# Four turned tiles of the adjacency matrix left unstored in the first stage and turned again by VectorE in the passes

## The reference

```python
h = relu(layernorm(x));  e = h + par * (diag * h) @ W            # W, diag, par: one set for users, one for items
x = x + layernorm(adj @ (adj.T @ e)) * gamma + beta + h          # layer 0
h = relu(layernorm(x));  x = x + adj @ h                         # layer 1
h = relu(layernorm(x))                                           # layer 2, Chebyshev, K = 3
t1 = adj @ h;  t2 = 2 * (adj @ t1) - h;  t3 = 2 * (adj @ t2) - t1
x = x + h @ w0 + t1 @ w1 + t2 @ w2 + t3 @ w3 + bias
h = relu(layernorm(x));  d = (sum(adj + I, axis=1)) ** -0.5      # layer 3
x = x + relu((d * (adj + I) * d) @ (h @ W + b))
```

## Time and profile before

| | us |
|---|---|
| median of three runs | 1450.97 |
| the profiled execution, its own time | 1449.24 |
| its span, first to last instruction | 1447.0 |
| TensorE matmul busy | 1419.3 (98%) |
| VectorE busy | 491.5 (34%) |
| ScalarE busy | 399.7 (28%) |
| GpSimd busy | 84.2 (6%) |
| DMA, bytes moved | 523.26 MB, mean 362 GB/s |

### The profile page before, as it was taken

How to read it: one execution, slowest core, us unless ns; L and a number is a source line. 1 busy time by engine, 2 the same in 40 slices (tenths; PEclk the granted TensorE clock), 3 DMA queues, 4 the chain that set the end, 5 groups by cost and what they waited for, 6 DMA issues and landing times.

```text
span 1447.0 us, 18473 instructions
## 1 busy us (share of the span) xinstructions
PE 1419.3 (98%) x7601; PEld 600.1 (41%) x7601; DVE 491.5 (34%) x1082; ACT 399.7 (28%) x885; POOL 84.2 (6%) x67
## 2 busy tenths in 40 slices
PE   6999999999999999999999999999999999999998
PEld 3555555555555563333333333333333333333332
DVE  6684544545546533331132211011311121101044
ACT  2378777777776551000000000000000000000000
POOL 2210000000000037000000000000000000000000
PEclk9999999999999999999999999999999999999999
DMA  9999999999999998999996797899797848996998
GB/s 322 392 417 411 420 412 414 419 408 415 401 406 372 388 403 348 419 421 420 420 413 217 315 361 291 327 350 319 302 340 263 311 180 354 393 382 224 357 420 315
DMA packets 97607, 523.26 MB, mean 362 GB/s; under 512 B 18764, under 2 KB 18804, under 8 KB 54644
## 3 DMA queue, kind: packets, MB, share of 16 engines
q1 hardware_dynamic: 90436, 520.40, 91.3%
q10 hardware_dynamic: 7088, 1.67, 0.5%
HBM read 415.88 MB, written 106.17 MB: 361 GB/s over the span
## 4 chain that ended last, share of the span: by engine, by line
PE 61%; DMA 2%; DVE 1%; POOL 0%; issue 0%; ACT 0%; DVEq 0%
PE turned L640 33%; PE acc L640 25%; DMA over_wide<-adj_t 2%; PE turned L673 1%; PE turned L825 1%; PE t_rows L809 0%; PE turned L831 0%; DVE staged L1169 0%; PE t_acc L799 0%; PE t_acc L725 0%; PE t_rows L725 0%; POOL rstd L1272 0%; DVE staged L1035 0%; DVE staged L1025 0%; DVE staged L1231 0%
## 5 line engine op out<-in xcount | busy, mean ns | idle before, releaser
L1129 DVE STREAM_TRANSPOSE staged<-raw 32x256 f32<-32x256 f32 x448 | 194.9, 435 | 5.8
L651 PE MATMUL t_acc<-raw,E 128*64 128x384 f32 (+1 forms) x1120 | 184.4, 476 | 5.7 <-DMA raw<-in_adj_dram 5.7
L879 ACT ACTIVATE staged<-turned 128x512 f32<-128x512 f32 x303 | 152.7, 640 | 105.7 <-PE turned L673 105.2
L923 ACT ACTIVATE t_t<-raw 128x768 uint8<-128x768 f32 (+1 forms) x216 | 177.2, 902 | 0.0
L640 PE MATMUL acc<-staged,t_cur 128*64 128x512 f32 x720 | 161.1, 596 | 0.0
L673 PE MATMUL turned<-ident,raw 128*128 128x128 f32 x1376 | 160.2, 274 | 0.0
L673 PEld LDWEIGHTS turned<-ident,raw 128*128 128x128 f32 x1376 | 149.7, 140 | 24.9 <-issue 24.9
L640 PE MATMUL turned<-over_last,C 128*64 128x512 f32 x672 | 152.1, 592 | 0.0
L651 PEld LDWEIGHTS t_acc<-raw,E 128*64 128x64 f32 x1120 | 78.3, 138 | 109.4 <-issue 86.0
L1272 POOL TENSOR_TENSOR rstd<-rstd,minus_half 128x8 f32<-128x8 f32 (+1 forms) x30 | 44.2, 1473 | 1267.1 <-DVE rstd L1031 1267.1
L640 PE MATMUL turned<-over_last,R 128*64 128x512 f32 x512 | 116.5, 593 | 0.0
(11 more groups left out here) (139 smaller groups left out, 1062.9 us busy)
## 6 DMA issues: line engine op xcount, KB each, us to landing
over_last<-adj_t SPq DMA_DIRECT2D x181, 1024.0 KB, 8.9
staged<-adj_t SPq DMA_DIRECT2D x91, 1024.0 KB, 9.5
raw<-in_adj_dram SPq DMA_DIRECT2D x60, 1536.0 KB, 19.7
adj_t<-staged SPq DMA_DIRECT2D x30, 3072.0 KB, 18.1
over_wide<-adj_t SPq DMA_DIRECT2D x23, 1024.0 KB, 7.6
raw<-in_adj_dram SPq DMA_DIRECT2D x10, 1024.0 KB, 14.8
adj_t<-over_last SPq DMA_DIRECT2D x8, 1024.0 KB, 12.1
adj_t<-C SPq DMA_DIRECT2D x2, 1024.0 KB, 21.7
```

The lines of the kernel that those rows point to most:

```text
L651: last = nc.tensor.matmul(t_acc[h * D:(h + 1) * D, 0:columns], E[:, m * SUB + a, :], raw_of(g, m)[:, a, h * columns:(h + 1) * columns], st ...
L879: nc.scalar.activation(turned_into(g, u)[:, i * B:(i + 1) * B], turned[n % TURN_BANKS][:, :], ACT.Copy) \
L923: nc.scalar.activation(passed[n % 2][:, 0:chunks(g) * P], raw_of(g, m)[:, a, :], ACT.Copy, accum_out=deg_part[:, m * SUB + a, g:g + 1]).th ...
L1129: last = nc.vector.transpose(dst[b * SQ:(b + 1) * SQ, :, :, q * SQ:(q + 1) * SQ], src[q * SQ:(q + 1) * SQ, :, :, c * P + b * SQ:c * P + (b ...
```

## The change

Four tiles, `UNSTORED`, are left out of the stores: the stores of pairs (3, 3), (3, 4), (4, 1) and (5, 3) write 2 MB in place of 3 MB, and no longer wait for VectorE's turn of that pair. In the passes these tiles are needed twelve times. Each time, four DMAs of the sync queue load the raw block from the input matrix, in pieces of 512 bytes, 1 MB together, into `over_wide`, which is no slot any more (the raw room). VectorE turns it from there into the tile's slot with 16 transposes of 32 by 512 in four quarters. `place_turning` puts the quarters behind steps of the plan: from the step after the slot comes free, and not in the three steps (four in passes 0 and 3) behind a row's end. The raw load stands in the sync queue at least eight steps of slot use ahead of the slot's release, and from the second on waits until the one before is turned. `AT_START` has seven slots in place of eight, and the tiles rotate through one slot less. The order of the 500 products is the same.

The diff, without `place_turning`'s assertion and the lines that only pass names on:

```diff
-AT_START = [0] + list(range(EARLY_SLOTS + NB, SLOTS)) + [ONCE] + list(range(EARLY_SLOTS + NB - KEPT, EARLY_SLOTS + NB))
+AT_START = list(range(EARLY_SLOTS + NB, SLOTS)) + [ONCE] + list(range(EARLY_SLOTS + NB - KEPT, EARLY_SLOTS + NB))
...
+UNSTORED = [(3, 11), (4, 11), (1, 14), (3, 17)]
+ROOM_BLOCKS = 2 * CH
+QUARTERS = 4
+ROOM_LANDS, ROOM_AHEAD = 6, 8
...
-                loads_of[j] = loads_of.get(j, 0) + 1
-                self.slot[n], self.load_no[n] = j, loads_of[j]
-                self.loads.append(n)
+                self.slot[n] = j
+                if self.tiles[n][1:3] in UNSTORED:
+                    self.turned_no[n] = len(self.turned_no) + 1
+                else:
+                    loads_of[j] = loads_of.get(j, 0) + 1
+                    self.load_no[n] = loads_of[j]
+                    self.loads.append(n)
...
+    def place_turning(self):
...
+        row_ends = {s + i for s, r in self.ended.items() for i in (1, 2, 3, 4) if i < 4 or self.rows[r][0] in WEIGHED}
+        self.rooms_before, self.quarters_in, end = {}, {}, 0
+        for n in self.turned_no:
+            free = step_of[self.slot_before[n]][-1]
+            asked = max(end + 1, free - ROOM_AHEAD)
+            after = next(x for x in self.loads if self.slot_before[x] is not None and step_of[self.slot_before[x]][-1] >= asked)
+            self.rooms_before.setdefault(after, []).append(n)
+            s = max(free + 1, end + 1)
+            while sum(products[asked:s]) < ROOM_LANDS:
+                s += 1
+            for q in range(QUARTERS):
+                while s in row_ends:
+                    s += 1
+                self.quarters_in.setdefault(s, []).append((n, q))
+                end = s
+                s += 1
...
+        room_raw = over_wide[0][:, :].rearrange("p (b k) -> p b k", k=P)
...
             def store(g, m):
-                wait_copied(sp, g, m)
-                at = g * CHUNKS * PAIR
-                sp.dma_start(adj_t[m, :, at:at + STAGE_WORDS], staged_pair(g, m)).then_inc(stored_by(g, 2 * m)[0], 16)
+                at, words = g * CHUNKS * PAIR, STAGE_WORDS
+                if (m, (g + 1) * CHUNKS // 2 - 1) in UNSTORED:
+                    words = STAGE_WORDS - TILE_WORDS
+                    sp.wait_ge(chunk_copied, COPIED_NO[g, m, words // B - 1])
...
+                sp.dma_start(adj_t[m, :, at:at + words], staged_pair(g, m)[:, 0:words]).then_inc(stored_by(g, 2 * m)[0], 16)
...
+            def load_room(n):
+
+                p, m, k, dual = plan.tiles[n]
+                if plan.turned_no[n] > 1:
+                    sp.wait_ge(room_turned, plan.turned_no[n] - 1)
+                for c in range(2):
+                    for h in range(2):
+                        at = (2 * c + h) * SUB
+                        sp.dma_start(room_raw[:, at:at + SUB, :],
+                                     pair_v[:, m, h, :, (2 * k + c) * P:(2 * k + c + 1) * P]).then_inc(room_in, 16)
...
-            first_load(next(first))
...
             for n in plan.loads[len(AT_START):]:
+                for x in plan.rooms_before.get(n, []):
+                    load_room(x)
                 sp.wait_ge(multiplied, plan.used_no(plan.slot_before[n]))
                 load_turned(n)
...
+            def turn_room(n, q):
+
+                if q == 0:
+                    dve.wait_ge(room_in, 64 * plan.turned_no[n])
+                    dve.wait_ge(multiplied, plan.used_no(plan.slot_before[n]))
+                tile = whole[plan.slot[n]].rearrange("p (b n) -> p b n", n=P)
+                for b in range(4):
+                    last = nc.vector.transpose(tile[b * SQ:(b + 1) * SQ, :, q * SQ:(q + 1) * SQ],
+                                               room_raw[q * SQ:(q + 1) * SQ, :, b * SQ:(b + 1) * SQ])
+                if q == QUARTERS - 1:
+                    last.then_inc(room_turned, 1)
...
+                for n, q in plan.quarters_in.get(s, []):
+                    turn_room(n, q)
```

More of the change, by code:

```diff
@@ L200, in __init__ @@
         loads_of = {}
+        self.turned_no = {}
         for n in range(len(self.tiles)):
@@ L205, in __init__ @@
                 _, j, self.slot_before[n] = place
-                loads_of[j] = loads_of.get(j, 0) + 1
-                self.slot[n], self.load_no[n] = j, loads_of[j]
-                self.loads.append(n)
+                self.slot[n] = j
[5 more added lines that the diff above has]
+                    self.loads.append(n)
                 if j != ONCE:
                     empty.append((self.used_no(n), j, n))
+        self.place_turning()
+    def place_turning(self):
+        step_of = {}
+        for s, n in enumerate(self.step_tile):
+            for x in [n] * (n is not None) + self.duals_in.get(s, []):
+                step_of.setdefault(x, []).append(s)
+        products = [(n is not None) + len(self.duals_in.get(s, [])) for s, n in enumerate(self.step_tile)]
+        row_ends = {s + i for s, r in self.ended.items() for i in (1, 2, 3, 4) if i < 4 or self.rows[r][0] in WEIGHED}
[14 more added lines that the diff above has]
+                s += 1
+            assert end < step_of[n][0], (self.tiles[n], end, step_of[n])
     def early_in_row(self, order, m, left, step, ready, covered):
@@ L323, in gnn_stack @@
         weights_ready = sem("weights_ready")
+        room_in = sem("room_in")
+        room_turned = sem("room_turned")
         x_in = [sem(f"x_in{i}") for i in range(len(X_PARTS))]
@@ L373, in gnn_stack @@
         adj_v = adj_d.rearrange("(m a p) k -> p m a k", a=SUB, p=P)
+        pair_v = adj_d.rearrange("(m a h p) k -> p m h a k", a=SUB, h=2, p=P)
         x_v = x_d.rearrange("(t p) d -> p t d", p=P)
@@ L414, in wait_loaded @@
         def wait_loaded(eng, n):
-            if n in plan.load_no:
+            if n in plan.turned_no:
+                eng.wait_ge(room_turned, plan.turned_no[n])
+            elif n in plan.load_no:
                 eng.wait_ge(whole_in[plan.slot[n]], 16 * plan.load_no[n])
@@ L567, in store @@
             def store(g, m):
-                wait_copied(sp, g, m)
-                at = g * CHUNKS * PAIR
-                sp.dma_start(adj_t[m, :, at:at + STAGE_WORDS], staged_pair(g, m)).then_inc(stored_by(g, 2 * m)[0], 16)
+                at, words = g * CHUNKS * PAIR, STAGE_WORDS
+                if (m, (g + 1) * CHUNKS // 2 - 1) in UNSTORED:
+                    words = STAGE_WORDS - TILE_WORDS
+                    sp.wait_ge(chunk_copied, COPIED_NO[g, m, words // B - 1])
+                    if (g, m, MOVED_BANK) in MOVED_NO:
+                        sp.wait_ge(bank_moved, MOVED_NO[g, m, MOVED_BANK])
+                else:
+                    wait_copied(sp, g, m)
+                sp.dma_start(adj_t[m, :, at:at + words], staged_pair(g, m)[:, 0:words]).then_inc(stored_by(g, 2 * m)[0], 16)
             def store_kept(u):
```

## The result

The changed kernel takes **1467.8 us** (median of 4 runs, 1465.3 to 1470.0), the kernel before 1451.4 us beside it (1450.4 to 1452.0): a ratio of 1.0115, 95% interval 1.0103 to 1.0127. It is 16.4 us slower; forecast were 8.5 us, and the range ended at 1466.5. The profiled execution took 1466.71 us with a span of 1464.9 us, 17.9 us more than the span before.

The account below looks back on a forecast made before the run. TensorE, busy 98% of the span, was taken as the bound, with DMA mattering at three full stretches. Terms -6.0 + 4.1 + 4.7 + 3.2 + 0.7 + 1.8 = +8.5 us gave 1459.5 us, range 1450.5 to 1466.5.

Parts of the forecast that it names:

- first stage: Four stores 1 MB shorter take away TensorE's remaining waits for raw blocks from 337 us on: -6.0 us (-5 to -6.5).
- start of the passes, waits: One more load in the chain and the raw room, less an earlier last store, delay tile (1, 9): +4.1 us (1.5 to 6).
- weighing, waits: Three quarters of transposes ahead of VectorE's reads make TensorE wait: +4.7 us at row (0, 4), +3.2 at row (0, 3).
- small delays: Three further turns end 0.5 to 1 us into a row's end in passes 2 and 3: +0.7 us (0 to 2).
- tail: With 14 slots in place of 15 the last loads wait for one release more: +1.8 us (0 to 3).
- The three surpluses behind it: Excess lengths of the first stage's last pairs, 1.16, 0.55 and 1.07 us, all counted as saved.
- The missing load at 490 us: Without the load into `over_wide` the last store lands earlier at the start of the passes: -1.4 us.
- The room: Raw room's four DMAs ahead of the load for (1, 9): 3.5 us, between bounds of 2.5 and 4.7.
- The first rival: Transposes priced by instruction, not by columns, about 0.44 us each: -3.2 us in sum, 1447.8 us; chance 0.1.
- the turn that I had called the tightest: Turn of (3, 17): room lands about 673 us, turn ends before row (0, 2)'s end at 684.8, by under a microsecond.
- Dearer pieces and dearer squares: Rival: raw room costs 4.7 us and transposes near 0.87 us, +15 in sum, 1466 us; chance 0.15.
- the saved megabytes don't reach TensorE: Rival: raw blocks wait for turns, not DMA, so the first stage stays; +14 in sum, 1465 us; chance 0.08.

Follow-up runs that it names:

- e5: Kernel before with twelve small reductions on VectorE ahead of the weighing's first-batch reads in rows (0, 3) and (0, 4), four ahead of the second's; 1458.68 us against 1450.86.
- e2: Changed kernel with three unstored tiles, (1, 14) stored and loaded again, so no raw room ahead of tile (1, 9); 1462.81 us against 1450.45 for the kernel before.
- e1: Changed kernel with quarters kept out of the nine steps behind a row's end in pass 0; 1458.33 us against 1450.45 for the kernel before.
- e4: Changed kernel with one quarter fewer ahead of the weighing's first-batch reads in pass 0; 1458.83 us against 1450.45 for the kernel before.
- e12: Kernel before with all 25 stores of groups one to five shortened by 1 MB, those tiles loading the neighbour's; 1439.58 us against 1451.1.
- e8: Changed kernel with raw rooms filled from the stored matrix in 2 KB pieces, not from the input in 512-byte pieces; 1465.66 us against 1450.45 for the kernel before.
- e7: Kernel before with only the four stores shortened by 1 MB, those tiles loading the neighbour's; 1445.53 us against 1450.86.
- e3: Changed kernel with nothing unstored: whole stores, no raw room, no turning, only one slot less; 1454.06 us against 1450.86 for the kernel before.
- e9: Changed kernel with three unstored tiles (without (1, 14)), slot 0 back early and after the last turn, pass 0 quarters moved later; 1447.24 us against 1450.96 for the kernel before.
- e6: Kernel before with eight small VectorE reductions ahead of the weighing's first-batch reads in rows (0, 3) and (0, 4); 1451.84 us against 1450.86.
- e10: e9 with (2, 17) as a fourth unstored tile; 1454.34 us against 1450.96 for the kernel before.

## Why the prediction was wrong

The sign, the places and most of the waits were right; the size was off by 9 us (17.6 by the profile against 8.5; by the medians 16.4), and the largest part of that is a term that the sum lacked. The table's measured column is one profiled execution.

| step | predicted | measured |
|---|---|---|
| first stage | -6.0 | -4.2 |
| start of the passes, waits | +4.1 | +3.8 |
| weighing, waits | +7.9 | +8.2 |
| small delays | +0.7 | +0.4 |
| tail | +1.8 | +3.1 |
| half clock behind the waits | none | +6.4 |

**The failed step: waits were priced at their own length.** "Both waits hold TensorE itself, with all its products behind", I wrote, and added 4.7 and 3.2 us; at the start of the passes I added 4.1. I had read a granted clock of 1.00 in every window and took it for a constant. TensorE had never paused for more than 1.0 us there. Three pauses of 3.4, 3.3 and 4.9 us brought three stretches at half clock, which cost 1.6, 1.6 and 3.1 us. Shown by e5 (a wait of 3.3 us made by reductions alone brings 1.7 us more), by e2 and e1 (without the wait no half clock at its place), and by e4, where a wait of 2.0 us at row (0, 4) brought 1.7 more. That a wait stops the products behind it was right; that it costs no more than its length was not.

**First stage.** Pairs of 14.97 us from 337 us on: right up to 446 us, with 3.1 us gained of the 3.3 that I had summed there. The three surpluses behind it, 1.16, 0.55 and 1.07, I counted in full; 1.2 us came of 2.8. My premise "the first saved megabyte covers six pairs at 0.4, so the saving is there ahead of the waits" failed: the queue ran short in between and lost the lead. That it is bytes that bind, e12 shows. Three other profiles of the same stage code gave 4.1 us (e8), 3.3 (e1) and 1.5 (e4), so a single execution tells this term only within 1 to 3 us; and e7, with the same four stores shortened, gave 5.0 us from 337 us on and 5.3 by the medians. So the term was too large, but by less than the -4.2 of one profile makes it look.

**Start of the passes.** The sum was right, its parts not. The missing load at 490 us gave back 1.8 us against the products and not 1.4, in e3 2.0, so that the slot costs next to nothing there. The room cost 3.45 us against my 3.5, which I had picked between bounds of 2.5 and 4.7; that it came so near is in part luck. The rule of the Trainium skill, DMA: Bandwidth & Descriptors, Specifications, that pieces of 512 bytes and more run at line rate would have given 2.5. The traces don't agree: the room took 3.45 us in 512-byte pieces and 2.67 us in 2 KB pieces, each with four DMAs, where a tile's load takes 2.49. The other rooms agree: in each of the two kernels ten of the twelve landed behind a full queue, in 3.42 to 3.55 and in 2.58 to 2.70 us. So 0.8 us a megabyte is the price of the pieces (with the other source, as said), and 0.2 that of four DMAs in place of one.

**Transposes and weighing.** A transpose of 32 by 512 took 703 ns; 701 was worked out from the slope of the earlier trace rows. The waits came at 3.3 and 4.9 us against 3.2 and 4.7. The first rival, priced by instruction, is out. The turn that I had called the tightest, of (3, 17), held by 0.5 us; its room landed at 667.0 us and not at 673, and what it waited for was its slot, until 669.95.

**Tail.** The mechanism held and the size was off: 3.1 in place of 1.8 us. e3 gives 2.2 of it to the slot alone, and e9, where the slot comes back after the last turn, has no wait there. But the term scatters: with the slot missing the last products lost 1.7 (e8), 2.5 (e1), 2.6 (e4), 3.1 (changed kernel) and 4.2 us (e2), and in e5 and e6, which have the slot, 0.6 and 0.9. So the difference between 1.8 and 3.1 is within what single executions show, and its cause stays open.

**The rivals.** "Dearer pieces and dearer squares" gave 1466 us and "the saved megabytes don't reach TensorE" 1465, both near the result, and both for reasons that did not occur: 3.45 and not 4.7 us for the room, 0.70 and not 0.87 for the transpose, and a stage that did gain. A number that fits is no evidence for its cause.

## What to carry to other kernels

Price a new wait of a TensorE that has run without pause at its length and, from about 2 us on, at up to 3 us more for the clock; and when a change must make such waits, it should keep each short: among the products no wait of up to 1.8 us brought the half clock. Work that fills an engine's idle time goes behind the read that another engine waits for, not ahead of it, even if the idle time is there: the turns cost 13 us (8.2 of waits and 4.8 of half clock) when three quarters stood at steps five to seven behind a row's end, and 2.4 us when moved past step nine. DMA time saved ahead of need is kept only if the queue has a load that is allowed to start.

## What was not expected of the hardware

The granted clock fell behind these waits of TensorE, all among the products of the passes: 2.0 (e4), 2.6 (e8), 2.9 (e10, tile (2, 11)), 3.0 (e10), 3.3 (e5, and row (0, 3) of the changed kernel), 3.4 to 3.5 (tile (1, 9) in three profiles) and 4.9 us. It did not behind 0.5 (e4), 0.9 (e6) and 1.8 us (e5). Length alone doesn't decide: in the first stage it stayed at full behind waits of 1.5 (changed kernel, e1), 1.6 (e2, e6, e9) and 2.0 us (e4), the last as long as one that brought the half clock in the same execution. What else decides, no run tells. The stretch at half clock was 3.4 or 6.8 us, and the same wait brought either: at row (0, 3), after 3.3 us, 3.4 in the changed kernel and 6.8 in e2, where it began while TensorE was still waiting. All fourteen stretches go by this: in the seven of 6.8 us the clock fell 0.5 to 1.2 us before the wait ended, in the seven of 3.4 us at its end or up to 1.2 us behind it. So such a wait has no fixed price, only a range: 1.6 to 2.7 us behind the one of 3.4 to 3.5 us at tile (1, 9).

The sync queue was held for 7.8 us at the third of four DMAs with 512-byte pieces (9.3 us in e10's first room) and 0.4 us with 2 KB pieces. It came only behind other transfers: at the changed kernel's two rooms that were issued into an idle queue, at 765 and 1261 us, none of the four DMAs took over 0.51 us. It cost nothing here; whether it would ahead of an urgent load, no run tells.
